# Layer 3's opening taken apart: offsets, first hats and first products moved among layer 2's last steps

## The chip, the cores and the metric

One core of a Trainium2 chip runs the whole program in one launch. The metric is device time in microseconds (us). The kernel before takes 521.72 us, the median of three runs (521.71 to 522.06).

## The reference

A batch x of 16 images, 64 channels of 16 by 16 pixels, passes through four residual layers, all in float32 (the normalization ahead of each layer and the additions are the kernel's; what they compute is this):

```
x = x + L0(norm(x))    # 1x1 convolutions, group norms, a gate of six basis functions
x = x + L1(norm(x))    # a state-space layer: depthwise 3x3, an outer-product state, layer norm
x = x + L2(norm(x))    # attention: 8 heads of 8 channels over 256 positions
x = x + L3(norm(x))    # deformable 3x3 convolution
```

Layer 3 is the one that the change is about. A 3x3 convolution gives, for each of nine taps, an offset (dy, dx) and a mask for each pixel. Each tap samples the image at its shifted place, bilinearly, times sigmoid(mask); a 64x64 matrix for each tap mixes the channels, and the nine results are summed. Bilinear weights are hats: max(0, 1 - |position - row|) for the 16 rows, and the same for the 16 columns.

## The kernel before, in words

Two images lie beside each other on the 128 partitions, so that x is eight pairs of [128, 256]. Engines run from their own instruction lists and wait on semaphores; the order of the work is written out by hand. A layer is one block, and all engines meet at its end.

**Layer 2** (line 768) walks steps v from -19 to 143 (`ROWS`). Step v asks for the largest scores of step v+19 (`largest`: two products on PE into one of three ring banks, one reduction of 0.69 us on DVE), the scores of step v on PE (`scores`), their exponents on ACT (line 972, 128x512), and parts of the context sums (line 1074). An image has eight steps. The last `largest` is at v = 108; from v = 109 the step holds only scores, exponents, context and, once in eight steps, the turning, normalizing, projecting and adding of one image (lines 1085 to 1096, 925 to 940). From v = 128 only the last two images' ends are left. GpSimd (POOL) splits the maxima in bf16 parts, and SP sends them back into the stacks by DMA, four small ones for each image.

**Layer 3** (line 1119) has an opening and a main loop. The opening normalizes all of x (GroupNorm, lines 140 to 159), pads the images on DVE (line 1310), sends them by DMA into a stack of shifted copies, and convolves four groups of four images (`conv_offsets`, line 1469: 24 products and four with a grid of pixel positions each). Offsets and masks of group 0 are spread over the partitions by PE (`to_places`, lines 1482 and 1487) for the first two thirds of the taps, and go through DRAM (stores 1164 and 1168, loads 1175 and 1180) for the last third and for all later groups. Hats are made in chunks of four images, each in three thirds of 128x768: distance and hat on ACT (1386, 1392), times the mask (1203 to 1207), and split in three bf16 parts, each a cast and a subtraction (1401, 1215, 1406, 1221). DMAs of SP gather the parts as `hats` (line 1243). Meanwhile six pairs of products (`weigh`, line 1501) multiply the first image pair by the tap matrices, copied out by DVE (1321) and ACT (1418).

The main loop has 72 steps, nine taps for each of eight pairs. In step v PE spreads the rows' hats of v+1 (line 1510) and the columns' of v+2 (line 1520), in six steps of nine does a `weigh` for the next pair, and samples (line 1533). ACT copies the columns (1414), DVE multiplies (1345). Hats of the next chunk are made one ACT operation a step, in twelve steps (`hat_steps`, line 1426), chunk 1 from step 0, chunk 2 from step 18, chunk 3 from step 36; POOL does the masks and subtractions. The hats of a chunk are first wanted by `spread_cols` two steps ahead of its first step. SP's list is in order: for a chunk it waits for its parts, sends the hats of the first pair, then loads the next chunk (nine DMAs), then sends those of the second pair.

## Time and profile before

| | us |
|---|---|
| median of three runs | 521.72 |
| the profiled execution | 520.96 |
| its span, first to last instruction | 519.2 |
| PE busy in the span | 439.2 (85%) |
| DVE busy | 341.0 (66%) |
| ACT busy | 291.8 (56%) |
| POOL busy | 133.0 (26%) |

The mean granted TensorE clock is 0.921 of full speed. In the profile's strip of 40 equal slices (13 us each), PE's busy tenths are 9 in nearly all of layer 2 and of layer 3's main loop; the slices that stand out are those of the openings of layers 1, 2 and 3. A busy share is an average of stages with different limits, and an engine's idle time costs nothing unless the end waits for it.

### The profile page before, as it was taken

The numbers are of one execution on the slowest core, as the hardware profiler recorded it, in microseconds if no ns is written. First come the engines' busy times: TensorE is split into PE (matmuls) and PEld (weight loads), VectorE is DVE, ScalarE is ACT, GpSimd is POOL, SyncE is SP. The second block draws the span as 40 slices with busy tenths as digits, with TensorE's granted clock in tenths as the row PEclk, the third lists the DMA queues.
The fourth block names the chain that finished last, engine by engine and source line by source line (L and its number), as shares of the span: only waits on it lengthen the run. The fifth ranks groups of instructions, "written<-read, shape, count | busy, mean of one in ns | idle before, by whom it ended". The sixth has DMA issues, their size and how long they took to land. (4 is left out here: it accounts for less than half of the span.)

```text
span 519.2 us, 9486 instructions
## 1 busy us (share of the span) xinstructions
PE 439.2 (85%) x3462; PEld 235.8 (45%) x3462; DVE 341.0 (66%) x664; ACT 291.8 (56%) x515; POOL 133.0 (26%) x162
## 2 busy tenths in 40 slices
PE   6328766999999988579999999947978999999997
PEld 6116545655455654323344333323534544454443
DVE  3558876233353568978999999142564778788786
ACT  1579945131523437038778888822875668487432
POOL 4510004000000004844432211113354528146000
PEclk9857998999999998558999999986997999999999
DMA  5600000900000002971210000008292390741600
GB/s 144 167 1 1 0 0 0 200 2 1 1 0 1 0 1 65 268 237 44 83 43 2 4 3 3 3 0 202 80 227 48 70 206 1 178 98 43 155 11 12
DMA packets 20895, 33.81 MB, mean 65 GB/s; under 512 B 5784, under 2 KB 15624, under 8 KB 20084
## 3 DMA queue, kind: packets, MB, share of 16 engines
q1 hardware_dynamic: 16852, 23.70, 19.1%
q0 software_dynamic: 2176, 6.35, 4.4%
q10 hardware_dynamic: 1824, 3.19, 2.4%
q8 instruction: 27, 0.44, 0.4%
q14 instruction: 16, 0.13, 0.1%
HBM read 16.21 MB, written 4.64 MB: 40 GB/s over the span
## 5 line engine op out<-in xcount | busy, mean ns | idle before, releaser
L1345 DVE TENSOR_TENSOR L_s<-L_row_ps,L_cols 128x1024 f32<-128x1024 f32 x72 | 87.6, 1218 | 7.1 <-PE L_row_ps L1510 6.5
L917 DVE TENSOR_REDUCE L_mx<-L_ring 128x2 f32<-128x512 f32 x128 | 83.3, 686 | 11.1 <-PE L_ring L1041 10.5
L972 ACT ACTIVATE L_e<-L_ring 128x512 f32<-128x512 f32 x128 | 73.7, 597 | 20.9 <-PE L_ring L1054 18.9
L1533 PE MATMUL L_acc<-L_s,L_t_sb 128*64 128x256 f32 x576 | 79.5, 398 | 1.4 <-DVE L_s L1345 1.2
L1414 ACT ACTIVATE L_cols<-L_col_ps 128x512 f32<-128x512 f32 x72 | 42.8, 596 | 48.9 <-PE L_col_ps L1520 48.6
L1041 PE MATMUL L_ring<-stacks_k_st,stacks_q_st 64*128 64x256 bf16 x256 | 50.9, 301 | 6.5 <-DVE L_v_all L906 4.6
L1533 PEld LDWEIGHTS L_acc<-L_s,L_t_sb 128*64 128x64 f32 x576 | 35.5, 138 | 35.2 <-DVE L_s L1345 20.9
L1054 PE MATMUL L_ring<-stacks_q_st,stacks_k_st 64*128 64x256 bf16 x256 | 47.2, 282 | 1.2 <-DMA stacks_q_st<-L_m_parts 1.2
L1510 PE MATMUL L_row_ps<-L_hats,L_sel 48*128 48x512 bf16 x144 | 43.6, 384 | 0.0
L1074 PE MATMUL L_ctx_ps<-L_e,L_v_x 128*32 128x256 f32 x512 | 41.1, 395 | 0.0
L1321 DVE COPY L_t_sb<-L_acc 128x192 f32<-128x192 f32 x48 | 17.1, 357 | 30.6 <-PE L_acc L1501 30.6
L1041 PEld LDWEIGHTS L_ring<-stacks_k_st,stacks_q_st 64*128 64x128 bf16 x256 | 16.0, 98 | 43.0 <-DVE L_mx L917 23.5
L385 PE MATMUL L_y<-L_t,all_w_post 128*128 128x256 f32 x96 | 24.8, 412 | 12.0 <-DVE L_t L343 12.0
L1520 PE MATMUL L_col_ps<-L_hats,L_sel 48*128 48x512 bf16 x72 | 28.1, 392 | 6.8 <-DMA L_hats<-L_parts 6.8
L1501 PE MATMUL L_acc<-all_w_all,L_xn 64*128 64x192 f32 x96 | 26.8, 361 | 5.0 <-DVE L_t_sb L1321 2.7
L860 POOL MEMSET L_v_x<- 128x1024 f32 x1 | 1.0, 952 | 102.5 <-POOLq L503 102.5
L385 PEld LDWEIGHTS L_y<-L_t,all_w_post 128*128 128x128 f32 x96 | 19.2, 206 | 17.6 <-DVE L_t L343 14.9
L1207 POOL TENSOR_TENSOR L_hat<-L_hat,L_mask 64x768 f32<-64x768 f32 x9 | 16.3, 1816 | 40.1 <-ACT L_hat L1392 40.1
L1501 PE MATMUL L_col_ps<-all_w_all,L_xn 64*128 64x192 f32 x96 | 26.4, 357 | 0.0
L422 ACT ACTIVATE L_uu<-L_z,L_minus_mu,L_inv 128x256 f32 x48 | 24.4, 585 | 1.4 <-DVEq L315 1.4
L640 ACT ACTIVATE L_sq<-L_t_ps 128x1024 f32<-128x1024 f32 x4 | 4.1, 1024 | 34.9 <-PE L_t_ps L723 34.9
L1501 PEld LDWEIGHTS L_acc<-all_w_all,L_xn 64*128 64x128 f32 x96 | 18.5, 203 | 9.2 <-DVE L_t_sb L1321 4.3
(271 smaller groups left out, 829.5 us busy)
## 6 DMA issues: line engine op xcount, KB each, us to landing
L_hats<-L_parts SPq DMA_DIRECT2D x28, 216.0 KB, 4.9
L_hat<-L_offsets SPq DMA_DIRECT2D x20, 192.0 KB, 4.7
L_mask<-L_offsets SPq DMA_DIRECT2D x10, 192.0 KB, 4.9
stacks_q_st<-L_q_parts SPq DMA_DIRECT2D x12, 128.0 KB, 3.6
stacks_k_st<-L_k_parts ACTq DMA_DIRECT2D x12, 128.0 KB, 4.8
stacks_q_st<-L_q_parts POOLq DMA_DIRECT2D x12, 128.0 KB, 2.6
stacks_k_st<-L_k_parts POOLq DMA_DIRECT2D x12, 128.0 KB, 3.0
L_stack<-L_xpad SPq DMA_DIRECT2D x7, 162.0 KB, 5.6
```

The costliest lines, as they stand in the source:

```text
L385: mm = pe.matmul(y2[:, ds(k, 1), :], w_post[:], t[:, q, j:j + 1, :], start=False, stop=(j == NB - 1))
L917: dve.tensor_reduce(mx[:, n % 2, :, head], ring[:, place(step) % 3].rearrange("p (q s) -> p q s", q=2), AX.X, ALU.max).then_inc(max_read, 1)
L972: act.activation(e[:, k], ring[:, 3 + v % 3], ACT.Exp, scale=HD2 ** -0.5).then_inc(e_ready, 1)
L1041: mm = pe.matmul(ring[:, place(step) % 3, q * N:(q + 1) * N], rows_of(q_st, n, h, p)[:, q * P:(q + 1) * P], rows_of(k_st, n, h, p), start= ...
L1054: mm = pe.matmul(ring[:, 3 + v % 3, t * N:(t + 1) * N], rows_of(k_st, c, h, p)[:, t * P:(t + 1) * P], rows_of(q_st, c, h, p), start=True, ...
L1074: mm = pe.matmul(ctx_ps[32 * j:32 * j + 32, g * N:(g + 1) * N], v_x[:, c % 2, t, 4 * g + j, :], e[:, 4 * g + j, t * N:(t + 1) * N], start= ...
L1345: dve.tensor_tensor(s[:, q], row_ps[:, q], cols[:, t % 3:t % 3 + 1].broadcast_to([P, 2, 2 * N]), ALU.mult).then_inc(s_ready, 1)
L1414: act.activation(cols[:, v % 3], col_ps[:, c % 2], ACT.Copy).then_inc(col_read, 1)
L1501: mm = pe.matmul(out, xn[rows, b, k // 3 * P:(k // 3 + 1) * P], w_all[rows, k % 3 * TW:(k % 3 + 1) * TW], start=True, stop=True)
L1510: mm = pe.matmul(row_ps[:, v % 2, h], sel[0:3 * H, h], hats[0:3 * H, n % 2, :, t * N:(t + 1) * N], start=True, stop=True)
L1520: pe.matmul(col_ps[:, c % 2], sel[C:C + 3 * H, 2], hats[C:C + 3 * H, n % 2, :, t * N:(t + 1) * N], start=True, stop=True).then_inc(col_rea ...
L1533: mm = pe.matmul(acc[C * e:C * e + C, b, 0:N], t_sb[:, b, h, (KK * e + t) * C:(KK * e + t + 1) * C], s[:, q, h, e * N:(e + 1) * N], start= ...
```

## The change

Ten pieces of it are followed below; the diff is cut to them. The constants `to_places` shrink to three taps, and `l3_vec` gains two columns (1 + row, 1 - row) so that DVE can make a hat as min(1 + row - p, p + 1 - row), clipped at zero with the mask's product.

1. The padding buffers (`Pads`) are shared by layers 1 and 3 and cleared by POOL in layer 0.
2. Layer 3's normalization is split in two lots of four pairs. Lot 0 is done in layer 2 at v = 79 to 85, with exp(-0.5 ln(var)) on ACT. Lot 1 is done in the first two steps of layer 3's loop.
3. POOL pads groups 0 and 1, copies the selection matrix and normalizes pairs 0 and 1, between its maxima of images 12 to 14; SP sends both groups.
4. PE convolves group 0 at v = 109 to 115, spreads its first third at v = 117 and 121, and convolves group 1 in v = 122 to 135.
5. DVE makes the first third's hats and parts at v = 116 to 128; ACT makes masks by exponent and logarithm.
6. Thirds 1 and 2 come through DRAM (stores and loads by SP at the end of its layer 2 list). DVE makes the hats of third 1, ACT and POOL those of third 2.
7. The first pair's six `weigh` pairs go into v = 134 to 140, with their copies on DVE and ACT.
8. In layer 3, SP first stores group 1, sends third 2's hats once DVE's last subtraction (after sample 1) is done, loads chunk 1, and then sends the second pair's hats.
9. POOL pads groups 2 and 3 at the head of layer 3, and PE convolves them at steps 8 and 17 of the loop; ACT takes masks by Sigmoid one step later.
10. Chunks 1, 2 and 3 start at steps 2, 16 and 34. SP loads the next chunk ahead of sending a chunk's hats, and stores group 3 between the two pairs' hats of chunk 1.

```diff
 layer2, VectorE
+                    if v == 79:
+                        dve.wait_ge(signals.x_stats, 3 * NP + 4)
+                        opening.aggregate(dve, 0)
+                    if v == 83:
+                        opening.variances(dve, 0, a_ps[:, P:P + 4])
+                    if v == 85:
+                        opening.shifts(dve, 0)
+                    if v == 116:
+                        opening.take_offsets(dve, 0, ring[:, 2, 0:N])
+                    if v == 118:
+                        opening.below_by_vector(dve, 0, pos_ps)
+                    if v == 119:
+                        opening.hat_by_vector(dve, 0, pos_ps)
+                    if v == 123:
+                        opening.weigh_by_vector(dve, 0, mask_ps)
...
+                    if v == 129:
+                        opening.below_by_vector(dve, 1, opening.hat[:, 0, opening.cut(1)])
+                        opening.hat_by_vector(dve, 1, opening.hat[:, 0, opening.cut(1)])
+                    if v == 132:
+                        opening.weigh_by_vector(dve, 1, None)
+                    if v == 134:
+                        take_first_weighed(0)
+                    if v == 135:
+                        opening.take_rest(dve, 1)
+                    if v == 137:
+                        take_first_weighed(2)
+                        opening.take_last(dve, 1)
+                    if v == 141:
+                        take_first_weighed(4)
+                        opening.take_rest(dve, 2)
 layer2, ScalarE
+                    if v == 84:
+                        opening.scales(act, 0, a_ps[:, P + 4:P + 8])
+                    if v == 116:
+                        opening.take_masks(act, 0)
+                    if v == 131:
+                        opening.distance_by_scalar(act, 2)
+                    if v == 132:
+                        opening.hat_by_scalar(act, 2)
+                    if v == 133:
+                        opening.first_by_scalar(act, 1)
+                    if v == 135:
+                        take_second_weighed(0)
+                    if v == 136:
+                        opening.second_by_scalar(act, 1)
+                    if v == 138:
+                        opening.offsets_by_scalar(act, 1, ring[:, 0, 0:N])
+                        opening.take_masks(act, 1)
+                    if v == 139:
+                        take_second_weighed(2)
+                    if v == 140:
+                        opening.first_by_scalar(act, 2)
+                    if v == 142:
+                        take_second_weighed(4)
+                    if v == 143:
+                        opening.second_by_scalar(act, 2)
 layer2, TensorE
+        CONVOLVED_1 = {122: (0, 1), 124: (1, 2), 126: (2, 3), 131: (3, 4), 132: (4, 5), 135: (5, 7)}
...
+                    if 109 <= v < 116:
+                        if v == 109:
+                            pe.wait_ge(max_read, 126)
+                        opening.convolve(pe, 0, ring[:, 2, 0:N], v - 109, v - 108)
+                    if v == 117:
+                        pe.wait_ge(max_read, 8 * B)
+                        pe.wait_ge(m_read, B)
+                        opening.spread_positions(pe, pos_ps)
+                    if v == 121:
+                        pe.wait_ge(opening.hat_by_vector_done, 2)
+                        opening.spread_masks(pe, mask_ps)
+                    if v in CONVOLVED_1:
+                        opening.convolve(pe, 1, ring[:, 0, 0:N], *CONVOLVED_1[v])
+                    if v == 134:
+                        opening.wait_masked(pe, 0)
+                        pe.wait_ge(e_ready, 8 * B)
+                        weigh_two(0)
+                    if v == 137:
+                        weigh_two(2)
+                    if v == 140:
+                        pe.wait_ge(opening.first_read, 2)
+                        weigh_two(4)
 layer2, SyncE, after its last maxima
+                opening.store_offsets(sp, 0)
+                opening.store_masks(sp, 0)
+                sp.wait_ge(opening.stored[0], 32)
+                for j in (1, 2):
+                    opening.load_third(sp, 0, j, opening.first_mask)
+                for j in range(2):
+                    opening.send_first_hats(sp, j)
 layer3, SyncE
+                opening.store_offsets(sp, 1)
+                opening.store_masks(sp, 1)
+                opening.send_first_hats(sp, 2)
+                sp.wait_ge(opening.stored[1], 32)
+                for j in range(3):
+                    opening.load_third(sp, 1, j, mask[:, 1])
+                opening.send_hats(sp, 1, slice(0, TN), hats_in[1])
+                opening.send_group(sp, 3, opening.stack_in[3])
+                opening.store_offsets(sp, 2)
+                opening.store_masks(sp, 2)
+                for c in range(1, B // CH):
+                    if c < B // CH - 1:
+                        sp.wait_ge(opening.stored[c + 1], 32)
+                        for j in range(3):
+                            opening.load_third(sp, c + 1, j, mask[:, (c + 1) % 2])
                     sp.wait_ge(parts_ready, 3 * c + 3)
                     for b in range(2):
                         sp.wait_ge(s_used, KK * (2 * (c - 1) + b) + 10)
+                        opening.send_hats(sp, b, slice(0, TN), hats_in[b])
+                        if c == 1 and b == 0:
+                            opening.store_offsets(sp, 3)
+                            opening.store_masks(sp, 3)
 layer3, VectorE's loop
                         sample(n, t)
+                        if (n, t) == (0, 0):
+                            opening.variances(dve, 1, mean_ps)
+                        if (n, t) == (0, 1):
+                            opening.take_last(dve, 2)
+                            opening.shifts(dve, 1)
 layer3, ScalarE's and TensorE's loops
+CONVOLVED = {(0, 8): 2, (1, 8): 3}
+MASKED = {(1, 0): 2, (2, 0): 3}
+CHUNK_STARTS = {1: 2, 2: 16, 3: 34}
...
+                        if (n, t) in CONVOLVED:
+                            opening.offsets_by_scalar(act, g, acc[:, 1 - n % 2, 0:N])
+                        if (n, t) == (0, 1):
+                            opening.scales(act, 1, spread_ps)
+                            act.preload_act_table_set("sigmoid_and_others")
+                        for c, start in CHUNK_STARTS.items():
+                            h = KK * n + t - start
+                            if 0 <= h < len(hat_steps):
...
+                        if (n, t) in CONVOLVED:
+                            pe.wait_ge(first_read, 6 * n + 12)
+                            opening.convolve(pe, CONVOLVED[n, t], acc[:, 1 - n % 2, 0:N], 0, 7)
```

Some of the new functions that these lines call:

```diff
+    def variances(self, dve, n, mean):
...
+        dve.tensor_copy(self.mean[:, lot], mean).then_inc(self.norm_by_vector, 1)
...
+        dve.tensor_tensor(self.d[:, lot], self.mv[:, lot, 0], self.mean[:, lot], ALU.subtract).then_inc(self.norm_by_vector, 1)
...
+        dve.tensor_tensor(self.sp[:, lot], self.d[:, lot], self.d[:, lot], ALU.mult).then_inc(self.norm_by_vector, 1)
...
+        dve.scalar_tensor_tensor(out=self.var[:, lot], in0=self.sp[:, lot], scalar=EPS, in1=self.mv[:, lot, 1],
...
+    def take_masks(self, act, g):
...
+        act.activation(self.sig[:, g], self.off[:, g], ACT.Exp, scale=-1.0).then_inc(self.mask_own, 1)
...
+        act.activation(self.sig[:, g], self.sig[:, g], ACT.Ln, bias=1.0).then_inc(self.mask_own, 1)
...
+        act.activation(self.sig[:, g], self.sig[:, g], ACT.Exp, scale=-1.0).then_inc(self.sig_ready, 1)
...
+    def weigh_by_vector(self, dve, j, masks):
...
+        if j == 0:
+            dve.wait_ge(self.mask_spread, 1)
+            dve.scalar_tensor_tensor(out=rows[:, 0:2 * N], in0=rows[:, 0:2 * N], scalar=0.0, in1=masks[0], op0=ALU.max, op1=ALU.mult)
+            dve.scalar_tensor_tensor(out=rows[:, 2 * N:], in0=rows[:, 2 * N:], scalar=0.0, in1=masks[1], op0=ALU.max, op1=ALU.mult)
+        else:
+            dve.scalar_tensor_tensor(out=rows, in0=rows, scalar=0.0, in1=self.first_mask[:, self.cut(j)], op0=ALU.max, op1=ALU.mult)
+        dve.tensor_scalar(cols, cols, 0.0, None, ALU.max).then_inc(self.hat_by_vector_done, 1)
```

In layer 3's block, ACT's first operation on chunk 1 (`take_distance`, step 2) waits for the loads of that chunk, and its `take_first` (four steps on) for the hats of the pairs before to have landed, as it did before.

## Rows read from the trace of the kernel before

**Rows 1.** Busy time by stretch: us, each engine's busy time, granted clock, DMA share, GB/s.
```profile
340.00:345.00 5.00, 2.12 (x13) 1.23 (x12) 2.01 (x6) 0.87 (x2) 0.00 (x0) 1.00 0.00 0
...
420.00:440.00 20.00, 19.97 (x154) 10.05 (x152) 16.12 (x20) 17.07 (x31) 12.03 (x8) 1.00 0.37 74
```

**Rows 2.** Timeline: start, length, instructions; layer 2's last, the loop's first, the last.
```profile
344.45 0.43 DVE L940 BATCH_NORM_STATS2 all_x_bn<-all_x 128x6 f32<-128x256 f32 x1
...
380.63 2.35 DVE L1345 TENSOR_TENSOR L_s<-L_row_ps,L_cols 128x1024 f32<-128x1024 f32 x2 [1.13 <-PE L_row_ps L1510]
...
516.55 0.48 DVE L1349 SCALAR_TENSOR_TENSOR all_x<-L_acc,all_l_vec,all_x 128x256 f32<-128x256 f32 x1 [1.19 <-PE L_acc L1533]
```

**Rows 3.** Timeline of layer 2's tail: step 109's scores, one exponent, step 128's first product.
```profile
323.53 0.39 PE L1054 MATMUL L_ring<-stacks_q_st,stacks_k_st 64*128 64x256 bf16 x2
...
331.79 0.60 ACT L972 ACTIVATE L_e<-L_ring 128x512 f32<-128x512 f32 x1 [0.29 <-PE L_ring L1054]
...
338.60 0.33 PE L1090 MATMUL L_a_ps<-all_ident,L_ctx_n 128*128 128x128 f32 x1
```

**Rows 4.** Timeline of layer 3's opening: norm chain, spreads of positions and masks, one convolution.
```profile
346.99 0.17 DVE L148 TENSOR_TENSOR L_gn_var<-L_gn_sp,L_gn_mv 128x8 f32<-128x8 f32 x1
...
347.21 0.59 PE L169 MATMUL L_acc<-L_gn_var,all_avg 128*128 128x8 f32 x2 [0.66 <-DVE L_gn_var L148]
...
361.92 1.56 PE L1482 MATMUL L_row_ps<-L_off,all_to_places 128*128 128x256 f32 x6
...
363.42 1.08 PE L1487 MATMUL L_row_ps<-L_sig,all_to_places 128*64 128x256 f32 x4
...
367.89 2.80 PE L1473 MATMUL L_row_ps<-L_stack,all_w_off 128*32 128x256 f32 x48
```

**Rows 5.** Groups by line and form, 345 to 380 us: busy, mean ns of one, idle before.
```profile
L1215 DVE TENSOR_TENSOR L_rest<-L_hat,L_parts 128x768 f32<-128x768 f32 x3 | 2.9, 959 | 2.5 <-ACT L_parts L1401 2.4
...
L1321 DVE COPY L_t_sb<-L_acc 128x192 f32<-128x192 f32 x6 | 2.1, 352 | 3.3 <-PE L_acc L1501 3.3
...
L1406 ACT ACTIVATE L_parts<-L_rest 128x768 bf16<-128x768 f32 x3 | 2.5, 843 | 1.1 <-DVE L_rest L1215 0.9
...
L1375 ACT ACTIVATE L_sig<-L_row_ps,all_l_vec 128x256 f32<-128x256 f32 x4 | 1.9, 468 | 0.0
...
L1203 DVE TENSOR_TENSOR L_hat<-L_hat,L_row_ps 64x512 f32<-64x512 f32 x2 | 1.4, 675 | 8.2 <-ACT L_hat L1392 8.2
```

**Rows 6.** Timeline of layer 2's opening: one DVE cast, first with POOL idle, then beside POOL.
```profile
199.97 0.43 DVE L902 CAST L_parts<-L_e 128x512 bf16<-128x512 f32 x1
...
205.18 1.27 DVE L902 CAST L_parts<-L_e 128x512 bf16<-128x512 f32 x1
```

**Rows 7.** Timeline: chunk 1's first load issued, first used; third 2's hats used.
```profile
378.22 1.18 SPq L1175 DMA_DIRECT2D L_hat<-L_offsets  x2
...
382.12 0.93 ACT L1386 ACTIVATE L_hat<-L_hat,all_l_vec 128x768 f32<-128x768 f32 x1 [0.51 <-DMA L_hat<-L_offsets]
...
391.15 0.60 PE L1520 MATMUL L_col_ps<-L_hats,L_sel 48*128 48x512 bf16 x1 [2.32 <-DMA L_hats<-L_parts]
```

**Rows 8.** Timeline of DVE in the loop: samples 3, 4, 5, then 16 and 17.
```profile
385.72 1.22 DVE L1345 TENSOR_TENSOR L_s<-L_row_ps,L_cols 128x1024 f32<-128x1024 f32 x1
...
387.59 1.22 DVE L1345 TENSOR_TENSOR L_s<-L_row_ps,L_cols 128x1024 f32<-128x1024 f32 x1
...
392.54 1.22 DVE L1345 TENSOR_TENSOR L_s<-L_row_ps,L_cols 128x1024 f32<-128x1024 f32 x1
...
414.68 1.21 DVE L1345 TENSOR_TENSOR L_s<-L_row_ps,L_cols 128x1024 f32<-128x1024 f32 x1
...
417.86 1.21 DVE L1345 TENSOR_TENSOR L_s<-L_row_ps,L_cols 128x1024 f32<-128x1024 f32 x1
```

**Rows 9.** Busy time by stretch of one us, in and after the wait at 390.
```profile
394.00:395.00 1.00, 1.00 (x7) 0.66 (x6) 0.00 (x0) 0.27 (x1) 0.00 (x0) 0.50 0.01 5
...
398.00:399.00 1.00, 1.00 (x12) 0.55 (x9) 0.60 (x2) 0.90 (x3) 0.00 (x0) 1.00 0.00 0
```

More of the change, by code:

```diff
@@ L788, in layer2 @@
         xn = m.sb("xn", [P, NP, N])
-        parts = m.sb("parts", [P, 4, 2, 3, 2 * N], BF16)
+        parts = opening.shared[:, :].bitcast(BF16).rearrange("p (g s t n) -> p g s t n", g=4, s=2, t=3)
         k_st, q_st = stacks.k_st, stacks.q_st
@@ L853, in _ @@
                 load_stacks(sp, 1, 0)
-                with sp.Fori(0, NQ) as i:
+                with sp.Fori(0, NQ - 1) as i:
                     for j in range(4):
                         send_maxima(i, j)
+                for j in range(4):
+                    send_maxima(NQ - 1, j)
+                    if j < 2:
+                        opening.send_group(sp, j, opening.stack_in[j])
+                sp.wait_ge(s_ready, 8 * 12)
+                opening.store_offsets(sp, 0)
[5 more added lines that the diff above has]
+                    opening.send_first_hats(sp, j)
             @block.gpsimd
@@ L887, in _ @@
                         load_stacks(pool, g, 1, (2 * third, 2 * third + 2))
+                    if n in (12, 13):
+                        opening.pad_group(pool, x, n - 12)
+                    if n == 14:
+                        opening.copy_selection(pool)
+                        for p in range(2):
+                            opening.normalize_pair(pool, x, p)
+                opening.weigh_by_pool(pool, 2)
             @block.vector
@@ L940, in add, with take_first_weighed @@
                         dve.bn_stats(signals.x_bn[:, i, :], x[:, i, :]).then_inc(signals.x_stats, 1)
+                def take_first_weighed(k):
+                    for i in range(k, k + 2):
+                        opening.take_first_image(dve, 0, k + 1, i, weighed[0][i])
                 for v in ROWS:
@@ L990, in take_context, with take_second_weighed @@
                     act.activation(ctx[:, c % 2].rearrange("p g n -> p (g n)"), ctx_ps[:], ACT.Copy).then_inc(ctx_ready, 1)
+                def take_second_weighed(k):
+                    for i in range(k, k + 2):
+                        opening.take_second_image(act, 0, k + 2, i, weighed[1][i])
                 for v in ROWS:
@@ L1097, in project, with weigh_two @@
                     mm.then_inc(o_ready, 1)
+                def weigh_two(k):
+                    for i in range(k, k + 2):
+                        opening.weigh(pe, 0, 0, i, (weighed[0][i], weighed[1][i]))
                 for v in ROWS:
@@ new lines, with __init__ @@
+CONVOLVED = {(0, 8): 2, (1, 8): 3}
+MASKED = {(1, 0): 2, (2, 0): 3}
+CHUNK_STARTS = {1: 2, 2: 16, 3: 34}
+class ColumnTurns:
+    def __init__(self, kk):
+        order = [("cols", 0), ("cols", 1)]
+        for n in range(NP):
+            for t in range(kk):
+                if kk * n + t + 2 < kk * NP:
+                    order.append(("cols", kk * n + t + 2))
+                if t in WEIGHED and n < NP - 1:
+                    order.append(("t", n, t))
+        self.bank = {key: c % 2 for c, key in enumerate(order)}
+        self.count = {key: c + 7 for c, key in enumerate(order)}
@@ new lines, in layer3 @@
+        w_all, vec = weights.named("w_all l3_vec")
+        hat, rest, parts, hats, xn, sel, off, sig = (
+            opening.hat, opening.rest, opening.parts, opening.hats, opening.xn, opening.sel, opening.off, opening.sig)
+        t_sb, cols = opening.t_sb, opening.cols
+        mask, s = m.sb("mask", [C, 2, TN]), m.sb("s", [P, 2, 2, 2 * N])
+        row_ps, col_ps, acc = m.ps("row_ps", [P, 2, 2, 2 * N]), m.ps("col_ps", [P, 2, 2 * N]), m.ps("acc", [P, 2, 2 * N])
+        mean_ps, spread_ps = acc[:, 1, N + TW:N + TW + 4], acc[:, 1, N + TW + 4:N + TW + 8]
@@ L1229, in layer3 @@
+        row_ready, s_ready, s_used, added = m.sems("row_ready s_ready s_used added")
         with nc.Block() as block:
@@ L1420, in norm @@
                 def norm(n):
-                    act.wait_ge(col_ready, 15 * n - 23)
-                    act.activation(xn[:, n % 2, :], x[:, n, :], ACT.Identity, scale=gn.scale[:, n:n + 1], bias=gn.shift[:, n:n + 1]).then_inc(xn_ready, 1)
+                    act.wait_ge(col_ready, turns.count["t", n - 3, WEIGHED[-1]] if n > 2 else 6)
+                    opening.wait_shifted(act, n // 4)
+                    act.activation(xn[:, n % 2, :], x[:, n, :], ACT.Identity, scale=opening.scale[:, n:n + 1], bias=opening.shift[:, n:n + 1]).then_inc(xn_ready, 1)
@@ L1570, in _ @@
                         if v + 2 < KK * NP:
-                            spread_cols(v + 2, c)
+                            spread_cols(v + 2)
+                        if v == 0:
+                            opening.means(pe, 1, mean_ps)
                         if t in WEIGHED and more:
```

684 lines of the change are left out of this document (363 added, 321 removed).

## The prediction

> **What bounds the kernel now.** I read the strip of 40 slices first, then the busy time by stretch, then the timeline from the end of layer 2 to the first steps of layer 3's loop. The reader is to see two stretches that PE fills and a hole between them. In the loop PE is busy 19.97 of 20 us [rows 1]. Between the last statistics of layer 2, which end at 344.88, and the loop's first sample product at 380.63 lie 35.75 us [rows 2]. There PE, ACT, DVE and DMA wait for one another in turn: normalization, stack, convolution, spread, hats, split, gather. The tail of layer 2 is two things. From step 109 (323.53) to step 128 (338.60) ACT waits 0.29 us for PE's scores in its steps [rows 3], so PE sets the pace and whatever PE is given there lengthens it, while DVE is nearly free. After 338.60 all engines are mostly idle: PE has 2.12 us of work in 5 [rows 1].
>
> So the change can win at most those 35.75 us. What it wins is that hole, less what the same operations cost where they are put now.
>
> **The change part by part.** The times below are on the profile's own axis, and every sum is a shift against it. The profiled execution took 520.96 for a span of 519.2; the median, 521.72, is 2.5 above the span, and I add the shift to the median.
>
> *Lot 0's normalization (v = 79 to 85).* DVE gets four aggregations, four small operations and one for the shifts, each 0.17 or less [rows 4], PE two products of 8 columns, 0.59 at the opening's lower clock [rows 4], ACT two small ones. PE needs the variances that DVE makes only after its step's reduction and addition. I take 1.6: two products of about 0.35 at full clock, and 0.9 in which PE waits for DVE's four operations. Bounds 0.5 (only the products) and 3 (each handover drains the pipeline).
>
> *Padding, sending, normalizing of pairs 0 and 1.* These are on POOL and SP, whose lists in layer 2 hold only the maxima. A maximum has about ten steps from reading to use, and four added DMA issues take some 2.5 us of SP. I put the cost at 0; if a maximum came late, PE would wait up to one group of issues, 2.5 us.
>
> *PE in steps 109 to 127.* Group 0's convolution 2.8, positions 1.5, masks 1.1 for four passes and half as much for two more, so 1.5, and three of group 1's six parts, 1.4 [rows 4]. All 7.2 count, since PE sets the pace. Step 128 then starts at 338.6 + 1.6 + 7.2 = 347.4. ACT's three mask operations (0.47 each [rows 5], 1.6 with their waits on each other) lie beside PE's spread.
>
> *The tail behind them.* This is now a chain over DVE, ACT and PE. DVE ends the addition of image 13 at about 344.3, and then has in order: the first third's mask products (0.68, 0.41 and a clip), cast, normalization of image 14, subtraction, cast, subtraction; third 1's two hat operations, an addition, two mask operations, the last normalization, two copies of 0.35, and third 1's subtraction. With 0.96 for a subtraction or a hat of 128x768 [rows 5], 0.68 for 64x512 [rows 5], 0.57 for a cast or clip (0.43 for 128x512 [rows 6], scaled) and 0.6 for a normalization, these 17 take 11.2, up to 355.5. From there the chain crosses to ACT: second part 0.84 [rows 5], context copy 0.28, offsets of group 1 0.47 and their masks 1.6, two copies 0.66, first part of third 2 0.84; DVE's subtraction 0.96; ACT's second part 0.84. That is 6.5 to 7, so the block ends at about 362.5. PE's six pairs of products, 0.43 a pair, lie beside this. The two thirds from memory: masks at 336, two stores and their landing 3 to 4, loads 3.9 from issue to use [rows 7], so about 344, before DVE asks for third 1 at 350. Layer 3 starts at 362.8, its first sample product comes at 364.2: **16.4 earlier than 380.63**. Bounds: with no more than the old end of layer 2 (344.9 - 338.6 = 6.3) behind step 128, the block ends at 353.7; with each of some 20 handovers 0.2 dearer, at 366.5.
>
> *The loop's first steps.* DVE gains lot 1's four operations (0.7), third 2's last subtraction 0.96, and a wait of about 1.4 for PE's product and ACT's two before the shifts: +3.1 between samples 0 and 2, with sample 3 behind it. The first hats of third 2 are no longer late, but the second pair's are: SP sends third 2 at about 368.6, loads chunk 1 in 5.8 (nine issues of 0.6), and then sends those hats, which land about 15 us after the first of these issues. In the kernel before, the first load at 378.22 and the product that waited for hats at 391.15 lie 12.9 apart [rows 7], with fewer hats ahead. `spread_cols(9)` wants them in step 7, at about 380, so PE waits some 3.5 us there. Before, the wait was in step 4: samples 4 and 5 are 4.95 apart instead of 1.87 [rows 8]. One replaces the other: 0.
>
> *Two convolutions inside the loop.* PE has no room there [rows 1], so 2 x 2.8 [rows 4] = +5.7 with their entry.
>
> *Chunks.* Samples 16 and 17 are 3.18 apart, not 1.87 [rows 8]: 1.3 us of waiting for chunk 1's hats, and the same at chunks 2 and 3. Chunk 1 now starts two steps later, so its wait grows by 2 x 1.87: +3.7. Chunks 2 and 3 start two steps earlier, so theirs go: -2.6. A wait of 5 us will also drop PE's clock: the 2.3 us one at 390 left it at half (0.50 at 394, 1.00 at 398 [rows 9]), and the samples after it were 2.4 us later than full speed gives. +2.4. (The wait in step 7 replaces one that dropped it too.)
>
> Shared padding (the memsets of 2.3 us at the opening ran beside the normalization chain) saves nothing more.
>
> Sum: -16.4 + 3.1 + 5.7 + 3.7 - 2.6 + 2.4 = -4.1, and 521.72 - 4.1 = **517.6**.
>
> One rule that speaks against the change: a DVE cast took 0.43 with POOL idle and 1.27 beside a POOL operation [rows 6]. The Trainium skill, page "SBUF — State Buffer", section "SBUF: two separate sides", says that the two engines share a port pair as an exclusive lock, held for a whole operation, for DVE's faster modes and its operations with two SBUF inputs. By that rule DVE's chain would wait once for POOL's mask product of third 2, which makes 518.5 or so; the trace's pair agrees with it, but whether the two meet is not seen here.
>
> **The rivals.**
>
> *A: the waits in the loop don't grow.* Chunk 1's chain is one ACT operation a step, and in the loop ACT is busy 17.07 of 20 us but POOL only 12.03 [rows 1], so its parts could catch up when PE stands in its convolution. Then 3.7 and 2.4 fall away: 517.6 - 6.1 = 511.5. Against it: ACT's list is in order, and in step 8 it waits for the convolution itself.
>
> *B: SP's order makes it slower.* For chunk 1, SP first waits for group 2's stored masks (step 9), then issues nine loads (5.8 us) and only then the hats of chunk 1's first pair. By my timeline, loads are issued from 397 to 403 and the parts are ready at 403.7, so the order costs nothing. From the point where the masks land later than about 398, each us counts, and the hats' data also queue behind the loads' (loads and hats together took the 12.9 us of [rows 7], of which I give the loads some 7). Price: up to 7 more in step 16, with chunk 2's first ACT operations behind it: 517.6 + 6 = 523.6, slower than before. For it: in the opening, too, hats behind loads were late [rows 7]. Against it: step 9's masks need only one product and two ACT operations.
>
> *C: the change moves the chain and doesn't shorten it.* If the tail's handovers each cost what they did in the opening, with casts delayed by POOL and PE at half clock (its work there is thin, some 7 us in 16, the share of [rows 1]'s first stretch), layer 2 ends 4 us later, at 366.5, and the time is 521.6: no change.
>
> **How the numbers follow.** Forecast 0.45, A 0.20, C 0.15, B 0.20. A difference under about 0.2% (1.0 us) can't be told from none. The forecast's own spread is 3 us either way, 514.6 to 520.6, nearly all of it faster; with A that makes 0.66 faster. C splits round zero, which gives 0.12 for the same, and the rest, with B, 0.22 slower. The range: A's end less 2 (509.5), up to B's (524).
>
> **What would show it right or wrong.** In the profile after: the first sample product at 362 to 367; step 109 to step 128 some 22 us long with PE full; ACT and DVE alternating in the last 12 us of layer 2; a gap on PE before `spread_cols(9)` and a larger one before `spread_cols(18)`, both ending at a DMA of hats, with granted clock 0.50 behind them; none at chunks 2 and 3; two 2.8 us convolutions at steps 8 and 17. I am wrong if the first sample product is later than 368, if the wait at chunk 1's hats is under 2 us or over 9, or if ACT's wait for chunk 1's loads in step 2 holds the samples for more than 2 us.

## The result and the profile after

The changed kernel takes 530.67 us (median of five runs, 529.98 to 533.86), the kernel before, beside it, 522.06: a ratio of 1.018, 95% interval 1.016 to 1.020. The prediction, 517.6 with a range from 509.5 to 524.0, was wrong in sign.

The profiled execution after took 533.86, the longest of its five, for a span of 532.1; that of before took 520.96 for 519.2. So the two traces show +12.9, of which the medians show +8.6. The sums below are made against the two traces; each run's own time stands with the experiments.

Timeline of DVE, kernel after: start, length, instruction; the last operation of layer 2's chain, then samples 0, 2, 7, 8, 10, 16, 17, 19, 22, 23, 25 (sample n is DVE's product in the loop's step n), and the last addition.
```profile
360.48 0.96 DVE L1507 TENSOR_TENSOR L3o_shared<-L3o_shared,stacks_k_st 128x768 f32<-128x768 f32 x1 [0.45 <-ACT stacks_k_st L1501]
...
364.29 1.23 DVE L1678 TENSOR_TENSOR L_s<-L_row_ps,stacks_q_st 128x1024 f32<-128x1024 f32 x1 [1.10 <-PE L_row_ps L1792]
...
371.52 1.22 DVE L1678 TENSOR_TENSOR L_s<-L_row_ps,stacks_q_st 128x1024 f32<-128x1024 f32 x1
...
384.36 1.22 DVE L1678 TENSOR_TENSOR L_s<-L_row_ps,stacks_q_st 128x1024 f32<-128x1024 f32 x1
...
391.71 1.21 DVE L1678 TENSOR_TENSOR L_s<-L_row_ps,stacks_q_st 128x1024 f32<-128x1024 f32 x1
...
400.94 1.23 DVE L1678 TENSOR_TENSOR L_s<-L_row_ps,stacks_q_st 128x1024 f32<-128x1024 f32 x1 [5.25 <-PE L_row_ps L1792]
...
412.15 1.22 DVE L1678 TENSOR_TENSOR L_s<-L_row_ps,stacks_q_st 128x1024 f32<-128x1024 f32 x1
...
420.81 1.21 DVE L1678 TENSOR_TENSOR L_s<-L_row_ps,stacks_q_st 128x1024 f32<-128x1024 f32 x1
...
429.16 1.22 DVE L1678 TENSOR_TENSOR L_s<-L_row_ps,stacks_q_st 128x1024 f32<-128x1024 f32 x1 [4.35 <-PE L_row_ps L1792]
...
434.74 1.21 DVE L1678 TENSOR_TENSOR L_s<-L_row_ps,stacks_q_st 128x1024 f32<-128x1024 f32 x1
...
441.35 1.21 DVE L1678 TENSOR_TENSOR L_s<-L_row_ps,stacks_q_st 128x1024 f32<-128x1024 f32 x1
...
447.37 1.22 DVE L1678 TENSOR_TENSOR L_s<-L_row_ps,stacks_q_st 128x1024 f32<-128x1024 f32 x1
...
529.46 0.48 DVE L1682 SCALAR_TENSOR_TENSOR all_x<-L_acc,all_l_vec,all_x 128x256 f32<-128x256 f32 x1 [1.19 <-PE L_acc L1818]
```
The first sample stands at 364.29 against 380.63 [rows 2]: 16.3 won, as predicted. Then there are gaps where an undisturbed step takes 1.88: before sample 2, before 8 (7.35), in the two steps with convolution 2 (8 to 10), before 17 (8.66; 3.18 in [rows 8]), at convolution 3 (17 to 19), and before 23 (6.61). The last addition is 12.9 later than in [rows 2]. The loop took 29.2 more than before.

Waits after, 360 to 450 us: engine, line, what it waited for; us in total, times, longest.
```profile
ACT stacks_k_st L1724 <- DMA stacks_q_st<-stacks_k_st: 10.9, 2, 5.6
PE L_col_ps L1803 <- DMA stacks_q_st<-stacks_k_st: 10.7, 2, 6.0
...
ACT L3o_off L1402 <- PE L_acc L1390: 7.9, 2, 4.4
...
ACT L3o_shared L1708 <- DMA L_mask<-L_masks: 5.0, 2, 2.7
```
In this kernel's names the hats' transfer is `stacks_q_st<-stacks_k_st`. It ends a wait of PE (`spread_cols`, L1803) before samples 8 and 17, and a wait of ACT (`take_first`, L1724) before samples 8 and 23: ACT may not overwrite parts that are still being sent. ACT's list is in order, so the copies that PE needs stand behind that wait.

SP's transfers after: start, length of issue, line, what, count.
```profile
370.82 1.23 SPq L1429 DMA_DIRECT2D L3o_shared<-L_offsets  x2
...
378.32 2.76 SPq L1526 DMA_DIRECT2D stacks_q_st<-stacks_k_st  x4
381.12 0.65 SPq L1364 DMA_DIRECT2D stacks_stack<-stacks_xpad  x1
...
404.53 1.20 SPq L1429 DMA_DIRECT2D L3o_shared<-L_offsets  x2
...
411.12 2.82 SPq L1526 DMA_DIRECT2D stacks_q_st<-stacks_k_st  x4
428.21 0.33 SPq L1417 DMA_DIRECT2D L_offsets<-L3o_off  x1
431.04 0.33 SPq L1421 DMA_DIRECT2D L_masks<-L3o_sig  x1
431.41 2.79 SPq L1526 DMA_DIRECT2D stacks_q_st<-stacks_k_st  x4
```
The last three rows are the third gap, before sample 23: chunk 1's second pair goes out at 431.41, behind two stores that wait for convolution 3.

Busy time by stretch after: us, busy time of PE, its weight loads, DVE, ACT, POOL; granted clock, DMA share, GB/s.
```profile
350.00:362.00 12.00, 5.57 (x57) 3.26 (x49) 10.40 (x19) 7.20 (x17) 1.80 (x1) 0.93 0.13 49
362.00:372.00 10.00, 8.88 (x36) 4.11 (x37) 4.85 (x13) 3.57 (x8) 0.32 (x1) 0.50 0.16 57
372.00:392.00 20.00, 14.07 (x82) 6.92 (x82) 8.67 (x13) 9.39 (x19) 8.57 (x11) 0.76 0.95 198
392.00:400.00 8.00, 8.00 (x75) 3.33 (x71) 2.15 (x2) 1.88 (x4) 1.01 (x1) 0.63 0.01 2
```
This is the pattern to learn: the DMA engines are nearly idle until 372, full until 392, idle again until 400. At 392 PE has work, but half of its clock (granted 0.50 until 398, which is 1.2 of 2.4 GHz), and in that time comes convolution 2, from 394.36.

### The profile page after: what moved, and what is told of

The parts are those of the page before. It is cut to its first block and busy times, and to the rows that moved or that the text cites. A ratio compares the mean times of both kernels' runs of the same rounds, so it can differ in the third digit from the quotient of the medians.

```text
span 532.1 us, 9460 instructions
## 1 busy us (share of the span) xinstructions
PE 446.3 (84%) x3454; PEld 237.9 (45%) x3454; DVE 343.7 (65%) x663; ACT 285.8 (54%) x514; POOL 126.8 (24%) x152
## 5 line engine op out<-in xcount | busy, mean ns | idle before, releaser
L1678 DVE TENSOR_TENSOR L_s<-L_row_ps,stacks_q_st 128x1024 f32<-128x1024 f32 x72 | 87.8, 1219 | 18.2 <-PE L_row_ps L1792 17.9
L1818 PE MATMUL L_acc<-L_s,stacks_k_st 128*64 128x256 f32 x576 | 84.6, 418 | 0.9 <-DVE L_s L1678 0.8
L1737 ACT ACTIVATE stacks_q_st<-L_col_ps 128x512 f32<-128x512 f32 x72 | 42.7, 595 | 52.5 <-PE L_col_ps L1803 52.4
L1818 PEld LDWEIGHTS L_acc<-L_s,stacks_k_st 128*64 128x64 f32 x576 | 37.2, 145 | 37.1 <-DVE L_s L1678 18.1
L1792 PE MATMUL L_row_ps<-stacks_q_st,L3o_sel 48*128 48x512 bf16 x144 | 46.7, 408 | 0.0
L1803 PE MATMUL L_col_ps<-stacks_q_st,L3o_sel 48*128 48x512 bf16 x72 | 30.3, 423 | 19.3 <-DMA stacks_q_st<-stacks_k_st 10.7
L1644 POOL TENSOR_TENSOR L3o_shared<-L3o_shared,L_mask 64x768 f32<-64x768 f32 x9 | 16.3, 1815 | 49.4 <-ACT L3o_shared L1714 49.4
L1540 PE MATMUL L_acc<-all_w_all,L3o_xn 64*128 64x192 f32 x84 | 23.1, 358 | 0.0
L1540 PE MATMUL L_col_ps<-all_w_all,L3o_xn 64*128 64x192 f32 x84 | 23.0, 356 | 0.0
L670 PE MATMUL L_xs_ps<-stacks_stack,L_w_tap 128*128 128x512 f32 x48 | 22.7, 601 | 0.0
```

What stands on the lines that cost most here:

```text
L1540: mm = pe.matmul(out[e], self.xn[rows, b, k // 3 * P:(k // 3 + 1) * P], w_all[rows, k % 3 * TW:(k % 3 + 1) * TW], start=True, stop=True)
L1678: dve.tensor_tensor(s[:, q], row_ps[:, q], cols[:, t % 3:t % 3 + 1].broadcast_to([P, 2, 2 * N]), ALU.mult).then_inc(s_ready, 1)
L1737: act.activation(cols[:, v % 3], col_ps[:, turns.bank["cols", v]], ACT.Copy).then_inc(col_read, 1)
L1792: mm = pe.matmul(row_ps[:, v % 2, h], sel[0:3 * H, h], hats[0:3 * H, n % 2, :, t * N:(t + 1) * N], start=True, stop=True)
L1803: pe.matmul(col_ps[:, bank], sel[C:C + 3 * H, 2], hats[C:C + 3 * H, n % 2, :, t * N:(t + 1) * N], start=True, stop=True).then_inc(col_read ...
L1818: mm = pe.matmul(acc[C * e:C * e + C, b, 0:N], t_sb[:, b, h, (KK * e + t) * C:(KK * e + t + 1) * C], s[:, q, h, e * N:(e + 1) * N], start= ...
```

## The experiments

Theory 1 (order): hats are late because of what SP's list puts ahead of them. Theory 2 (amount): after 372 the DMA engines are full whatever the order. Theory 3 (clock): PE's half clock at the loop's start and the convolutions are the loss. Times are medians; each ratio is to the kernel before, run beside it. The code under a heading is shortened to what was moved.

**Second pair's hats ahead of chunk 1's loads.**
```
+ opening.send_hats(sp, 1, slice(0, TN), hats_in[1])
  sp.wait_ge(opening.stored[1], 32)
  for j in range(3): opening.load_third(sp, 1, j, mask[:, 1])
- opening.send_hats(sp, 1, slice(0, TN), hats_in[1])
```


> One edit to the kernel after the change: SP sends the second pair's hats of chunk 0 ahead of chunk 1's nine loads, not behind them. Theory 1 (order): the hats that end the wait at sample 8 are late because their bytes stand behind those of the loads; with the order turned, the gap before sample 8 falls from 7.35 to about 1.9 (-5.5), PE's clock is not lost there and convolution 2 takes 2.8 instead of some 6 (-3.5); chunk 1's loads land some 4 later, of which ACT's waits for them take back 2 to 4. Time about 524 to 526 (ratio to the kernel before 1.004 to 1.008). Theory 2 (amount): the same bytes have to land before the loop can go on, whatever their order; the wait reappears at ACT's distances or at chunk 1's hats, and the time stays at 529 to 532. Theory 3 (clock and convolutions): the loop is late because PE starts it at half clock; the gap goes but the samples behind stay slow, 527 to 529.

534.46, ratio 1.025 (1.023 to 1.028): slower than the change itself, and above theory 2's range too. Theory 1 misses here. Sample 8 no longer waits (1.88), but the wait moved to ACT's first use of the loads (timeline of ACT in this run, with the idle time and its end in brackets):
```profile
383.34 0.94 ACT L1708 ACTIVATE L3o_shared<-L3o_shared,all_l_vec 128x768 f32<-128x768 f32 x1 [11.33 <-DMA L_mask<-L_masks]
```

**A chunk's first hats ahead of the next chunk's loads.** The order that rival B blamed.
```
- load_third(c + 1) for j in 0..2      # ahead of chunk c's hats
  send_hats(c, pair 0)
+ load_third(c + 1) for j in 0..2
  send_hats(c, pair 1)
```


> One edit to the kernel after the change: from chunk 1 on SP sends a chunk's first pair of hats ahead of the next chunk's loads, as the kernel before did. Theory 1 (order, the data half of rival B): chunk 1's hats are issued at the same time (SP waited 0.9 for the parts behind the loads) but no longer share the DMA engines with the loads: they land in about 4 instead of 8, the gap before sample 17 falls from 8.66 to about 4.5, and with a shorter wait PE's clock is lost for less, so convolution 3 is 1 to 3 shorter; chunk 2's loads land some 5 later, and ACT may wait for them in step 16, up to 4. Time 523 to 528. Theory 2 (amount): ACT's wait for chunk 2's loads takes all of it back, 529 to 532.

533.08, 1.021 (1.017 to 1.024), above both ranges. In its trace the gap before sample 17 falls only from 8.66 to 7.42, since the hats go out at 412.47, no earlier: chunk 1's parts were ready only then. Rival B's mechanism alone gains nothing.

**Group 3's stores behind chunk 1's second pair.**
```
- if c == 1 and b == 0:
+ if c == 1 and b == 1:
      opening.store_offsets(sp, 3); opening.store_masks(sp, 3)
```


> One edit to the kernel after the change: group 3's offsets and masks are stored after chunk 1's second pair of hats, not before. Theory 1 (order): SP stands at the store until convolution 3 is done (428.2), though the hats could go from sample 17 on (421); with the edit they go some 9 earlier, ACT's first parts of chunk 2 don't wait for them (5.6 in one place), and samples 22 to 25 take 5.6 instead of 12.6: -7, time about 523 to 525. Rival: what ACT waits for there is chunk 3's loads and hats together on the DMA engines, or the profiled wait is peculiar to that execution; then the time moves by less than 2, 528.5 to 531.

524.55, 1.0075 (1.005 to 1.010): 6.1 back of the 8.6 (5.4 if the two ratios are compared), in the range of theory 1. In its trace samples 22 to 25 are 1.88 apart, and all eight transfers of chunk 1's hats leave ahead of the stores:
```profile
407.00 14.66 SPq L1526 DMA_DIRECT2D stacks_q_st<-stacks_k_st  x8
423.42 0.33 SPq L1417 DMA_DIRECT2D L_offsets<-L3o_off  x1
```

**All three.**

> The three edits of order together (second pair's hats of chunk 0 ahead of chunk 1's loads; a chunk's first hats ahead of the next chunk's loads; group 3's stores behind chunk 1's second hats). Theory 1 (order): gains add up to some 5 to 7 at each place, less ACT's later loads: 511 to 516, faster than the kernel before. Theory 2 (amount): DMA moves some 3.9 MB between 371 and 391 in any order; 526 to 531. Theory 3 (clock at the loop's start and convolutions in the loop): the waits go but half clock until sample 5 and both convolutions remain: 517 to 522.

527.35, 1.011 (1.007 to 1.015): in theory 2's range, and no better than the third edit alone; ACT waits 11.4 for the loads, as in the first run. The further runs stand on the moved stores (524.55).

**ACT's hat operation ahead of the offsets that wait for convolution 2.** The three lines of `offsets_by_scalar` move behind the loop over `CHUNK_STARTS`.

> On top of the moved stores of group 3 (524.55, its profile is the measure here): in ACT's step the operation on chunk 1's hats is listed ahead of the offsets that wait for the convolution, not behind them. Theory (chain): chunk 1's parts are late (407.0) because ACT stands some 4 us at convolution 2's offsets in step 8 with the second hat operation of third 2 behind it, and POOL's six last operations of 1.65 can only then run; with the turn, POOL's third mask product comes at about 391.5 instead of 396.6, the parts are ready at about 404, and the gap before sample 17 falls from 9.05 to about 6, so 521 to 523. Rival (steps): ACT's one operation a step sets the chain's end, in step 13, whatever happens in step 8; the gap stays at 8 to 9 and the time at 524 to 526.

527.81, 1.011 (1.008 to 1.014), above both ranges. No gain; the gap before sample 17 is 9.22 (9.05 in the base), as the rival has it.

**Less traffic in the full stretch.**
```
+ wait stored[1]; load thirds 0, 1 of chunk 1
  send_first_hats(sp, 2)
- wait stored[1]; load thirds 0, 1, 2 of chunk 1
  send_hats(sp, 1, ...)
+ load third 2 of chunk 1
+ sp.wait_ge(s_used, 10)
  send_group(sp, 3, ...)
```


> On top of the moved stores of group 3: chunk 1's thirds 0 and 1 are loaded ahead of third 2's own hats (in the 365 to 370 in which DMA is nearly idle), the second pair's hats ahead of third 2's loads, and group 3's stack is sent only after sample 7, when DMA is idle again. Theory (amount): from 372 to 391 the DMA engines are busy all the time whatever the order; now 1.2 MB go ahead of this stretch and 0.6 MB behind it, at some 200 GB/s 5 to 8 us; ACT's wait for its loads and PE's for the hats between samples 4 and 9 (7.1, 3.6, 2.6, 4.1 in place of about 1.9 each, so some 9 us lost) shrink by 4 to 7; time 517 to 521. Rival (third 2's hats): they now go out at 369 behind the loads' bytes, land at about 377 instead of 374, and PE waits there for what it saves later: 523 to 526.

515.02, 0.988 (0.983 to 0.993): faster than the kernel before by 1.2%, and 2 below the theory's range. Samples 5 to 8 are 1.88 apart.

**Its two parts by themselves**: only the stack of group 3 later, only the loads earlier.

> On top of the moved stores of group 3 (524.55): only group 3's stack (0.63 MB) is sent later, after sample 7. Theory (amount): that is 3 us of the DMA engines' full stretch between 372 and 391, and the second pair's hats share the engines with it: -2 to -3, 521.5 to 523. Rival: the stack is issued behind the hats on the same queue and so costs them nothing: 524 to 526.

> On top of the moved stores of group 3 (524.55): only the order at the loop's start (thirds 0 and 1 of chunk 1 loaded ahead of third 2's hats, second pair's hats ahead of third 2's loads); group 3's stack stays where it was, behind them. Theory (amount): 1.2 MB move into the time in which DMA stood nearly idle, 5 to 6 us less of the full stretch after 372: 518 to 520. Rival: what gave the 9.5 us of the run with both was the stack's later sending; then this alone gives under 3: 522 to 525.

524.07, 1.004 (1.001 to 1.006), and 516.61, 0.989 (0.984 to 0.993). The stack behind the hats cost next to nothing, where theory 2 expected 2 to 3; the loads put into DMA's idle time give 7.9 of the 9.5, more than expected. So it is not the amount in the stretch as such: what pays is to put loads into the idle time ahead of it. The second of these edits also puts the second pair's hats ahead of third 2's loads; what that turn gives by itself was not run. One stretch, 366 to 374, with the moved stores alone (the base of both) and with the loads earlier:
```profile
366.00:374.00 8.00, 7.04 (x47) 3.03 (x43) 5.07 (x8) 3.08 (x6) 3.65 (x7) 0.87 0.41 119
```
```profile
366.00:374.00 8.00, 7.61 (x41) 3.47 (x37) 4.38 (x6) 4.04 (x8) 2.63 (x5) 0.65 0.96 226
```
The DMA share goes from 0.41 to 0.96 and the rate from 119 to 226 GB/s, with PE busy 7.04 and 7.61 us.

**Traffic, and two hat operations beside convolution 2.** Less traffic as above, ACT's hat operation ahead of the offsets, and a second hat operation in the same step.

> Both together, and two of ACT's operations on chunk 1's hats in step 8, beside convolution 2: 513 to 518, faster than the kernel before, if the amount on the DMA engines and the chain behind convolution 2 are the causes; 521 or more if PE's clock at the loop's start or the convolutions' own time are.

515.27, 0.988 (0.983 to 0.994): in the range, but the same as with less traffic alone, so nothing here speaks for the chain behind convolution 2 by itself. Its trace has the parts ready at 396.1, one step earlier, but the gap before sample 17 is 9.52: the hats now stand behind chunk 2's loads.

**The same, hats ahead of chunk 2's loads.**

> The kernel with less traffic at the loop's start and the two hat operations beside convolution 2 (515.27; parts of chunk 1 ready at 396.1, its hats issued behind chunk 2's loads from 397.0, gap before sample 17 of 9.52 where 1.88 is free), and now chunk 1's first hats ahead of chunk 2's loads. Theory (amount and order): DMA is full from 393 to 405 with loads 1.73 MB and hats 0.86 MB; with the hats first they land at about 402 to 403, the gap falls to 5 or 6, and as chunk 2's loads come later ACT may wait up to 3 in steps 16 to 18: 511 to 514. Rival (landing): a set of four hats takes its 6 us of issue and landing in any order, as in the run where only this order was turned (7.42 in place of 8.66): 514 to 516.

514.62, 0.986 (0.980 to 0.992). The gap falls to 5.22, as the theory had it, but the time hardly: it lies in the rival's range, the runs spread over 6.5 us, and the interval contains the ratio of the run before it.

**Hats by thirds.** On the kernel of 515.27; the waits on PE and ACT that belong to it are left out here.
```
+ for j in range(3):
+     sp.wait_ge(parts_ready, 4 + j)
+     opening.send_hats(sp, 0, opening.cut(j), opening.first_hats[j - 1] if j else hats_in[0])
+     opening.load_third(sp, 2, j, mask[:, 0])
```


> The same kernel (515.27) with chunk 1's first hats sent by thirds of three places, each as soon as its parts are ready (POOL's last parts come at about 391, 394 and 396), third by third between chunk 2's loads; PE waits for each third where it reads it (samples 18, 21, 24). Theory: the first third lands at about 397, before step 16 at 399, so the wait of 7.6 before sample 17 and the half clock behind it in convolution 3 (some 1.6) go: 505 to 509, faster than the kernel before by 2.5 to 3%. Rival: SP's issues (12 and 9 of some 0.65 each, 14 us) are now the bound, the third third lands only at about 408 and PE waits 2 to 4 before sample 23: 510 to 513.

507.74 (six runs), 0.973 (0.969 to 0.978): the fastest, 14.0 under the kernel before beside it (521.76), in the theory's range. SP's rows (first third, its loads, second third), then DVE at samples 16 to 18:
```profile
391.02 2.54 SPq L1526 DMA_DIRECT2D stacks_q_st<-stacks_k_st  x4
393.60 1.23 SPq L1429 DMA_DIRECT2D L3o_shared<-L_offsets  x2
...
395.57 2.52 SPq L1526 DMA_DIRECT2D stacks_q_st<-stacks_k_st  x4
```
```profile
399.10 1.22 DVE L1687 TENSOR_TENSOR L_s<-L_row_ps,stacks_q_st 128x1024 f32<-128x1024 f32 x1
...
400.98 2.50 DVE L1687 TENSOR_TENSOR L_s<-L_row_ps,stacks_q_st 128x1024 f32<-128x1024 f32 x2
```
The gap before sample 17 is gone (1.88), and PE has the full clock in convolution 3 (1.00 from 402 to 406). Samples 23 and 24 come 3.3 late, the wait that its rival named; the rival's time was not.

**The clock.**
```
+ pe.wait_ge(opening.off_ready, 2)
+ keep_clock(pe, avg2, ring[:, 0], 32)    # end of layer 2's list on PE; 12 in the next two
```


> On top of the moved stores of group 3: 32 products of 128x128 (0.118 each in the trace, 3.8 us) at the end of layer 2's list on PE, written to a place nobody reads, so that PE's idle time of 3.8 us ahead of the loop is filled and the granted clock stays at 1.00 there. Theory (amount): the first samples come up to 3 us sooner (samples 0 to 4 at full clock) and then wait for the same loads and hats until 390: no more than 1 us of gain, 523.5 to 525.5. Rival (clock): PE runs from 361 to 377 at half clock, which costs 4 to 5 us that nothing gives back: 519 to 521.

528.86, 1.012 (1.007 to 1.016). The trial failed: a product is two instructions in the trace, the 32 took 7.41 us, held layer 2's end and put the first sample at 369.28. Twelve were tried next:

> The clock once more, on top of the moved stores of group 3 (524.55): 12 of the products instead of 32, each two instructions of 0.116 as the last run's trace shows, so 2.8 us in PE's idle 3.8 us, ending before the block does. Theory (amount): the loop starts on time, samples 0 to 4 take about 8.6 instead of 9.9, and samples 5 to 8 wait for the same loads and hats: gain 0 to 1, 523.5 to 525.5. Rival (clock): the cold start costs 3 us or more that nothing gives back: 521.5 or less.

> The same 12 products in the fastest kernel so far (hats by thirds, 507.74), where the transfers at the loop's start no longer hold samples 5 to 7, only sample 8 by 1.5. Theory: samples 0 to 4 are 1.3 sooner and sample 8 waits about as much longer; 506.5 to 508. Rival (clock): 505 or less.

523.86, 1.005 (1.001 to 1.009), and 511.84, 0.984 (0.977 to 0.991): no gain clear of the noise in the first (0.7 in the medians), as theory 2 has it, and none in the second, which came out above its theory's range too. In the first trace the products hold layer 2's end again: the granted clock had already fallen (0.62 from 358 to 360), they ran from 360.93 to 364.32, and the first sample stands at 366.11, not 363.47. PE's row, and the stretch 362 to 376:
```profile
360.93 3.39 PE L182 MATMUL L_ring<-all_avg 128*128 128x128 f32 x24
```
```profile
362.00:376.00 14.00, 11.48 (x83) 6.34 (x82) 8.93 (x18) 5.59 (x10) 4.29 (x8) 1.00 0.28 83
```
The clock is 1.00 where the base had 0.50 until 368, samples 0 to 4 take 8.63 and not 9.91 us, and then ACT waits 7.6 for chunk 1's loads. In the second trace the products end in time, the first sample stands at 362.61 (362.89 in its base), samples 0 to 4 are as short (8.63), and the gap before sample 8 is 5.30 where it was 3.41. Theory 3 falls for the loop's start: against these bases the half clock costs 1.3 there, and the transfers take it back.

How long the half clock lasts differs from trace to trace, though PE's idle time ahead of the loop is much the same: until 368 in that base, until 377 in the profile after, where samples 0 to 4 took 12.40 us, 3.8 more than at full clock. Part of the spread of the times may come from there; that is not shown.

## Why the prediction was wrong

Its terms against the two traces (a stretch's length after, less that before):

| term | predicted | measured |
|---|---|---|
| first sample (opening) | -16.4 | -16.3 |
| samples 0 to 2 | +3.1 | +4.3 |
| samples 2 to 8: second pair's hats | 0 | +3.2 |
| samples 8 to 10: convolution 2 | +2.85 | +6.3 |
| samples 16 to 17: chunk 1's first hats | +3.7 | +5.5 |
| samples 17 to 19: convolution 3, clock | +2.85 +2.4 | +5.4 |
| samples 22 to 25 | not named | +7.0 |
| chunks 2 and 3 | -2.6 | -2.5 |
| sum | -4.1 | +12.9 |

**Right: the opening.** Step 128's first product was predicted at 347.4 and stands at 347.50; PE is busy 20.00 of 20 us from 330 to 350; the first sample was predicted at 364.2 and stands at 364.29. That both agree to 0.1 is partly luck: the runs with the same layer 2 have their first sample between 362.9 (hats by thirds) and 365.4 (a chunk's hats ahead of the loads). The tail, from step 128's product to the first sample, is 16.8 in this trace, as in the sum, and 16.8 to 17.1 in theirs; within it DVE's list of 17 operations ended at 356.5, not 355.5, and the part on ACT behind it was as much shorter. The rule that spoke against the change (the Trainium skill, page "SBUF — State Buffer", section "SBUF: two separate sides": the two engines' shared port pair is locked for a whole operation) had one place, and there the trace agrees: DVE's mask product of third 1 met POOL's. The two rows are DVE's and POOL's timeline after.
```profile
351.67 2.22 DVE L1474 SCALAR_TENSOR_TENSOR L3o_shared<-L3o_shared 64x768 f32<-64x768 f32 x1
```
```profile
351.27 1.80 POOL L1487 TENSOR_TENSOR L3o_shared<-L3o_shared 64x768 f32<-64x768 f32 x1 [18.45 <-ACT L3o_shared L1483]
```
POOL's ended at 353.07 and DVE's at 353.89, so 0.82 of its 2.22 lie behind POOL's end; two thirds of such a product, 64x512, take 0.68 alone [rows 5]. The chain had the room: the first sample did not come later than the sum without it. Chunks 2 and 3 went as predicted too.

**The step that failed is "Chunks".** It priced one wait per chunk, at the first pair's hats, and put the second pair's at nothing: it took SP's list as issue time alone. But SP's list puts group 3's stores, which stand until convolution 3 is done in step 17, ahead of chunk 1's second pair. The hats, which could go once PE had used sample 16 (at 422.6), went at 431.41, and ACT, whose parts they read, stood with all its copies behind it. That is +7.0, and moving the two stores gave back 6.1 in the medians and made samples 22 to 25 even. It is the largest miss but not the only one: with the stores moved the time is still 524.55, slower than before.

**The second failure is "one replaces the other: 0"** in the loop's first steps. The wait in step 7 was predicted at 3.5, from hats that land 15 us after the first load's issue; it took 5.5 over a step's time, and PE's product with these hats came 19.5 us after that issue (370.82 to 390.32). ACT's two waits for the loads, 2.7 and 2.4, which the sum had at nothing, made samples 4 and 7 late as well. The change had moved two stacks (0.63 MB each) from the opening into the same stretch: 3.96 MB passed from 372 to 392, where before 2.99 MB passed from 380 to 392.
```profile
DMA packets 1745, 3.96 MB, mean 198 GB/s; under 512 B 336, under 2 KB 848, under 8 KB 1744
```
```profile
DMA packets 1420, 2.99 MB, mean 249 GB/s; under 512 B 435, under 2 KB 627, under 8 KB 1419
```
That the stacks' bytes made the wait is not shown: group 3's sent later gave 0.5 in the medians, and group 2's was never moved. What the runs show is that the edit which issues loads into DMA's idle time gives 7.9 us back.

The wait left PE at half clock (0.50 from 388 to 396), and convolution 2, priced at full clock, fell into it: 6.3 more for the two steps, not 2.85. In the runs without that wait the two steps still took 3.1 more than before (5.98 for 2.92 with less traffic, at a granted clock of 1.00), so the convolution itself was sized within 0.3. I had written "the wait in step 7 replaces one that dropped it too" and not asked what would stand in the slow time: before, no convolution did.

**Left out of the sum: the half clock at the loop's start.** Samples 0 to 2 took 4.3 more than before, not 3.1. At full clock, in the last two trials, they took 5.1 where before they took 2.93, so the added operations cost 2.2; the other 2.1 go with the granted clock of 0.50 from 362 to 372.

**Rivals.** B's sign was right and its mechanism was not: turning its order gained nothing until the parts were early, and even then only in the gap. C is refuted by the first sample; the half clock that it feared from PE's thin work did not come either (0.93 from 350 to 362, with PE busy 5.57 of 12). A is refuted by three waits that grew. ACT's wait for the loads (5.0 in two places, 2.7 and 2.4) was more than the 2 that I had set as a limit; in the first run it grew to 11.3.

Open remains in part why the last clock trial is 4.1 above its base. Its trace is 3.5 longer, and 2.7 of that stand by sample 10. The second pair's hats landed 8.3 us after their issue, not 6.5 (medians), and the stack of group 2 went out beside them at 369.26, not 370.84. PE then stood longer before sample 8 and lost its clock; the base's stretch and this one's (granted clock third from the end of the row):
```profile
384.00:386.00 2.00, 2.00 (x44) 1.13 (x36) 0.41 (x1) 1.75 (x3) 0.91 (x1) 1.00 0.95 223
```
```profile
384.00:386.00 2.00, 2.00 (x11) 0.33 (x11) 0.51 (x2) 1.11 (x2) 0.71 (x1) 0.53 0.00 0
```
That the stack made the hats late was not tried. The executions of the edited kernels spread over 3 to 8 us, and only one of each has a trace.

## What to carry to other kernels

When work is moved out of a quiet stretch, its transfers land in a busy one: list, for each queue and each in-order engine, what now stands ahead of the thing that is waited for, stores that wait for compute above all. Sum the bytes that must land between DMA's last idle time and each wait, and fill the idle time first. A wait is not priced by its own length: ask what PE does in the half clock behind it.

## What the runs showed of the hardware

After 3.8 us of idle time (359.1 to 362.9) PE began the loop with a granted clock of 0.50, which stayed until about 377 though PE was busy 6.00 of 6 us from 366 to 372; in the run with the moved stores, after the same idle time, it was back at 1.00 from 369. With 12 products in the idle time it was 1.00 throughout (358 to 380 in the last trial). The same kind of hats, four transfers of 216 KB, took 5.6 us from issue to landing in the kernel before (380 to 392) and 8.9 after (372 to 392), with two stacks beside them.
